# Sums of squares of the second half on the matrix engine, and another order of variances, modulation parts and turns

## What is computed

```python
mod = (silu(c) @ wmod).reshape(2, 6, 1, 1024)          # wmod: 1024 x 6144
sa, ca, ga, sb, cb, gb = (mod[:, i] for i in range(6))  # ga, gb kept away from 0
h = layernorm(x) * (1 + ca) + sa        # mean and variance over the 1024 features
x = x + ga * attn(h)   # per feature: softmax over the 2 batch entries, scores summed over 2048 tokens
h = layernorm(x) * (1 + cb) + sb
x = x + gb * ffn(h)    # silu(h Wgate) * (h Wup), then Wdown; inner width 2752
```

## Time and profile before

| what | us |
|---|---|
| median of 3 runs | 2859.61 |
| lowest and highest run | 2858.69, 2861.7 |
| the profiled execution, its own time | 2868.16 |
| its span, first to last instruction | 2866.0 |
| statistics and modulation, to the start of L1502 | 191.5 |
| PE busy in the span | 2757.2 |
| POOL busy in the span | 157.8 |

### The profile page before, as it was taken

One profiled execution on the slowest core, in us unless ns is written; L12 is line 12 of the kernel. 1 busy time (PEld: TensorE's weight loads), 2 busy tenths in 40 slices (PEclk: granted clock), 3 DMA queues, 4 the chain that ended last, 5 costly groups with the idle time before them and its releaser, 6 DMA issues.

```text
span 2866.0 us, 32548 instructions
## 1 busy us (share of the span) xinstructions
PE 2757.2 (96%) x11784; PEld 2162.9 (75%) x11784; DVE 1547.6 (54%) x2063; ACT 1061.8 (37%) x1622; POOL 157.8 (6%) x206
## 2 busy tenths in 40 slices
PE   8996998989899999999999999999999999999999
PEld 3344877777688887788887788887788888888887
DVE  7787787664445453544453433333546545546444
ACT  4456455544333333333333211111434333333332
POOL 5300010000001101001100000000000000000000
PEclk9997999999999999999999999999999999999999
DMA  8573989888878888978887999999757667667655
GB/s 362 198 299 134 325 297 321 299 282 297 294 276 314 314 283 268 302 279 312 313 285 252 347 348 356 351 352 333 255 211 264 218 220 250 216 224 253 228 208 167
DMA packets 359711, 795.77 MB, mean 278 GB/s; under 512 B 25760, under 2 KB 154016, under 8 KB 350848
## 3 DMA queue, kind: packets, MB, share of 16 engines
q1 hardware_dynamic: 341648, 721.32, 71.8%
q0 software_dynamic: 17088, 59.78, 6.2%
q10 hardware_dynamic: 816, 12.58, 1.0%
HBM read 553.26 MB, written 240.32 MB: 277 GB/s over the span
## 4 chain that ended last, share of the span: by engine, by line
PE 88%; DMA 4%; DVE 3%; issue 2%; ACT 2%; SPq 1%; POOL 1%; DVEq 0%; ACTq 0%; POOLq 0%
PE ps L1547 18%; PE ps L1549 18%; PE ps L1548 18%; PE ps L1609 10%; PE ps L1610 10%; PE ps L1611 10%; PE ps L1426 3%; PE ps L1453 1%; DMA x_raw_P<-xr_dram 1%; DMA whl_dram<-w_lo_P 1%; DMA xbuf<-x 1%; PE ps L1509 0%; PE ps L1502 0%; DMA wm<-wmod 0%; POOL sq_pair L564 0%
## 5 line engine op out<-in xcount | busy, mean ns | idle before, releaser
L1547 PE MATMUL ps<-x_hi_P,w_slot 128*128 128x512 f32 (+1 forms) x1848 | 725.3, 392 | 23.9 <-ACT vv L783 11.8
L1549 PE MATMUL ps<-x_hi_P,w_slot 128*128 128x512 f32 (+1 forms) x1848 | 723.8, 392 | 0.0
L1548 PE MATMUL ps<-x_lo_P,w_slot 128*128 128x512 f32 (+1 forms) x1848 | 723.7, 392 | 0.0
L1609 PE MATMUL ps<-hh,w_hi 128*128 128x512 f32 (+1 forms) x1232 | 481.1, 390 | 3.2 <-DVE w_lo L1322 1.9
L1610 PE MATMUL ps<-hl,w_hi 128*128 128x512 f32 (+1 forms) x1232 | 480.8, 390 | 0.0
L1611 PE MATMUL ps<-hh,w_lo 128*128 128x512 f32 (+1 forms) x1232 | 480.0, 390 | 0.0
L1547 PEld LDWEIGHTS ps<-x_hi_P,w_slot 128*128 128x128 f32 (+1 forms) x1848 | 345.1, 187 | 105.0 <-ACT vv L783 13.0
L1549 PEld LDWEIGHTS ps<-x_hi_P,w_slot 128*128 128x128 f32 (+1 forms) x1848 | 344.8, 187 | 78.4
L1548 PEld LDWEIGHTS ps<-x_lo_P,w_slot 128*128 128x128 f32 (+1 forms) x1848 | 345.3, 187 | 77.6
L1322 DVE TENSOR_TENSOR w_lo<-w_raw,w_hi 128x1408 fp32r<-128x1408 f32 x112 | 181.8, 1624 | 211.8 <-ACT w_hi L850 211.8
L1547 PE MATMUL ps<-x_hi_P,w_hi 128*128 128x512 f32 (+1 forms) x616 | 246.1, 400 | 43.7 <-DVE x_lo_P L1130 10.0
(11 more groups left out here) (179 smaller groups left out, 2598.4 us busy)
## 6 DMA issues: line engine op xcount, KB each, us to landing
w_slot<-whl_dram SPq DMA_DIRECT2D x420, 512.0 KB, 6.0
w_raw<-wds_dram SPq DMA_DIRECT2D x64, 704.0 KB, 4.6
hl_raw<-h_dram SPq DMA_DIRECT2D x56, 768.0 KB, 7.0
h_dram<-hb SPq DMA_DIRECT2D x30, 1280.0 KB, 9.6
whl_dram<-w_hi SPq DMA_DIRECT2D x140, 256.0 KB, 3.4
whl_dram<-w_lo_P SPq DMA_DIRECT2D x140, 256.0 KB, 4.0
w_raw<-wdn SPq DMA_DIRECT2D x48, 704.0 KB, 5.0
hl_raw<-h_dram SPq DMA_DIRECT2D x28, 1024.0 KB, 10.5
```

The source lines that it names most:

```text
L1547: mm(bank, hi[:, w], x_hi[name][:, k, :], start=fresh and k == 0, stop=False, skip_group_check=not fresh)
L1548: mm(bank, hi[:, w], x_lo[name][:, k, :], start=False, stop=False, skip_group_check=not fresh)
L1549: ins = mm(bank, lo[:, w], x_hi[name][:, k, :], start=False, stop=k == KH - 1, skip_group_check=not fresh)
L1609: mm(bank, hi[0:n, w], hh[stage % 2][0:n, j, :], start=fresh and j == 0, stop=False, skip_group_check=not fresh)
```

## The change

In round 1 (`t` = 1) POOL no longer adds pairs of squared tiles. PE sums every squared feature tile itself: 8 matmuls a batch in place of 4, waiting for `sq_ready` and releasing ACT's buffers through `sq_pair_used`. Round 0 stays as it was. PE's list of round 1 is reordered: the variances of batch (0,0) stand right behind the means, and one part lies between each two batches (part 4, then 5, then 6), where before four parts stood ahead of the first batch and two between the second and the third. Behind the last batch come parts 7 to 11. Part 12 alone, in place of parts 12 to 15, stands ahead of the turns of groups 0 and 1.

```diff
@@ gpsimd
                     sum_tiles(1, 0)
                     add_squares(0, 0)
                     sum_tiles(1, 1)
-                else:
-                    add_squares(0, 0)
-                add_squares(0, 1)
-                add_squares(1, 0)
-                add_squares(1, 1)
+                    add_squares(0, 1)
+                    add_squares(1, 0)
+                    add_squares(1, 1)
@@ scalar, square()
-                        act.wait_ge(sq_added, t * (4 * NSQ) + (i * NSQ + j + 1))
+                        if t:
+                            act.wait_ge(sq_pair_used, t * (4 * NSQ) + (i * NSQ + j + 1))
+                        else:
+                            act.wait_ge(sq_added, i * NSQ + j + 1)
@@ tensor, variances()
                     for j in range(NSQ):
-                        pe.wait_ge(sq_added, t * (4 * NSQ) + (i * NSQ + j + 3))
+                        if t:
+                            pe.wait_ge(sq_ready, t * (4 * NSQ) + (i * NSQ + j + 1))
+                            for k in range(SQ_PER):
+                                ins = mm(ps_var[h], ones[:], sq[:, j % 2, k, :], start=j == k == 0, stop=j == NSQ - 1 and k == SQ_PER - 1)
+                            ins.then_inc(sq_pair_used, 1)
+                            continue
+                        pe.wait_ge(sq_added, i * NSQ + j + 3)
                         mm(ps_var[h], ones[:], sq_pair[:, j % 2, :], start=j == 0, stop=j == NSQ - 1).then_inc(sq_pair_used, 1)
@@ tensor, the list of round 1
                     means(1, 1)
-                    parts(0, range(4, GROUP[0]))
-                    parts(1, range(2))
                     variances(0, 0)
+                    parts(0, range(4, 5))
                     variances(0, 1)
-                    parts(1, range(2, 4))
+                    parts(0, range(5, GROUP[0]))
                     variances(1, 0)
+                    parts(1, range(1))
                     variances(1, 1)
-                    parts(1, range(4, GROUP[1]))
+                    parts(1, range(1, GROUP[1]))
 
             pe.wait_ge(eye_loaded, 16)
             pe.wait_ge(centred, 16)
-            parts(2, range(4))
+            parts(2, range(1))
             turn(0, ps_mod[0], ROWS[0] + ROWS[1], 0)
             turn(1, ps_mod[0], ROWS[0] + ROWS[1], ROWS[0])
-            parts(2, range(4, GROUP[2]))
+            parts(2, range(1, GROUP[2]))
             parts(3, range(GROUP[3]))
```

## The result

The changed kernel takes 2869.65 us (median of 8 runs, 2866.5 to 2871.43), the kernel before beside it 2862.18 (8 runs, 2858.69 to 2865.6, the three shown ahead among them): 7.5 us more. The ratio is 1.0022, with a 95% interval of 1.0013 to 1.0030. Slower, by a quarter of a percent: little, but the interval lies clear of 1.

A forecast was written before the change was run, and what follows sets the result against it. The matrix engine's work up to the modulation's end was taken as the bound: 191.0 without stall, plus 6.1 idle and 2.7 lower clock, gives 199.8 against 191.5. That is +8.3 us, 2867.9 from 2859.6; range 2859.0 to 2871.0.

The forecast's parts named there:

- Part 1, the sums: Round 1 sums of squares: four batches take 28.5 us on the matrix engine against 22.3, costing +6.2 us.
- Part 1, VectorE's time: Without GpSimd's additions, five slow VectorE multiplications speed up; the 5.7 us freed are no gain while VectorE is ahead.
- Part 2, the order: Reordered round 1: last batch ends at 129.8 against 134.2, first pair's store issued at 138.8 against 147.01.
- Part 3, the turns: Both turns move from behind part 15 to behind part 12: same 2.4 us of work, nothing saved on the matrix engine.
- The sum without a stall: With no tile late, the modulation ends at 191.0, 0.5 us sooner than before.
- Part 4, the collision: The 4 MB store delays tile 12 to 13.0 us after issue; the matrix engine idles 6.1 us before part 12.
- The reckoning by equal turns: If DMA engines alternate between queues by packet, tile 12 lands at 150.2: stall 3.1 us, +5.3 in all; not adopted.
- The clock: After the idle before part 12 the matrix engine's clock falls to 1.2 GHz, costing 2.7 us as before.
- B: Rival: milder collision, stall of 1 to 3 us or clock not lowered, +2 to +5.5 us; chance 0.17.
- C: Rival: tile 12 lands in time despite the store, nothing idles, clock stays, -0.5 us (2859.1); chance 0.13.
- D: Rival: second tile late or squares can't keep up with the matrix engine, 3 us or more on top; chance 0.07.
- E: Rival: path runs through VectorE, whose chain ends 6 to 8 us sooner; over 6 us faster (2853); chance 0.05.

The follow-up runs named there:

- experiment 1: Kernel before with only the round 1 sums of squares moved to the matrix engine, old order kept: +8.6 us, ratio 1.0028 against the kernel before.
- experiment 9: Changed kernel with the late store, GpSimd still adding round 1 pairs that nobody uses while ScalarE waits for them: +0.3 us, ratio 0.9998 against the kernel before.
- experiment 7: Changed kernel with the turns put back behind part 15: +7.1 us, ratio 1.0024 against the kernel before.
- experiment 6: Changed kernel with the turns ahead of part 12, in the idle gap: +5.7 us, ratio 1.0019 against the kernel before.
- experiment 3: Changed kernel with the first pair's 4 MB store in round 1 issued behind the last modulation tile: -1.6 us, ratio 0.9992 against the kernel before.
- experiment 4: Kernel before with the first pair's 4 MB store in round 1 issued behind the last modulation tile: -4.2 us, ratio 0.9985.
- experiment 8: Changed kernel with one of the store's two chunks (2 MB) issued behind the last tile: +2.4 us, ratio 1.0011 against the kernel before.

## Why the prediction was right

The forecast was 2867.9 against 2859.6, +8.3; measured, +7.5 (2869.65 against 2862.18: with eight runs in place of three the kernel before is itself 2.6 us higher). By the start of the means of `x_f` it is 7.8. The chain of steps held.

- **Part 1, the sums.** Forecast 28.5 us for four batches; they took 7.0 and three times 7.1 on the path (98.10 - 91.14, 129.94 - 122.88), 28.1. That the engine has no idle time to hide them is shown by experiment 1.
- **Part 1, VectorE's time.** Forecast to be worth nothing; experiment 9 shows it, for the kernel with the late store.
- **Part 2, the order.** Last batch at 129.9 (129.8), store at 139.45 (138.8). What the prediction left unsaid is that the order by itself gains 2.9 us of start: it hides GpSimd's first two additions behind a part (2.4 us) and drops the wait of 0.50 ahead of the turns. The change gives the first of these up by its first half.
- **Part 3, the turns.** Worth nothing as the change places them (experiment 7), 2.2 us of start in the gap (experiment 6). The 2.4 us that the prediction calls their work hold the 0.50 of waiting shown in the earlier trace rows; they take 1.9.
- **The sum without a stall.** Forecast 191.0, and 190.51 in experiment 3: the batches took 0.4 less, the turns 0.5 less, the 20 parts 0.5 more than reckoned.
- **Part 4, the collision.** Tile 12 landed 13.0 us after its issue, as taken from tile 16; idle 6.26 (6.1). That close a hit is partly luck: with store and tile placed the same, it took 12.9 in experiment 6 and 14.3 in experiment 7, where the idle of 7.60 lies beyond the upper bound of 6.5. Tile 13 landed at 157.2 (157), without a second stall. The reckoning by equal turns, 150.2, was too early: it landed at 153.5. Experiments 3, 4 and 8 show the store as the cause.
- **The clock.** 5.67 - 3.45 = 2.2 us in place of 2.7: the term that was sized too high, by a fifth. The lowered stretch was shorter after the restart, 153.6 to 158 in place of 161.2 to 166.
- **A slip in the signs to look for.** "L1464 with 16 records only" should be 32: round 0 keeps 16 matmuls, and each is two records. The after trace has 32 there and the 64 of the new line.

The rivals: B's milder stall is what experiment 8 makes, C's schedule is what experiment 3 makes by moving the store away, and ends at 190.51 against the 191.0 of that case; with the store in place it did not come. D and E did not come.

## What to carry to other kernels

Before work is moved to the engine on the critical path, write down that engine's gapless sum: here it rose to within 0.5 us of the old total by the forecast, and within 1.0 as measured (190.51 against 191.47), with every wait removed, so next to nothing could be gained. When a reordering moves a large store, lay its issue beside the issues of the small ring transfers: their distance and the number of steps of slack decide about a stall, whatever the engines' shares say. A bulk store with no early reader belongs where the transfers beside it have slack (here 4 to 9 us on the median for one moved store: 4.2 in the kernel before, 4.6 on top of the order, 9.1 in the changed kernel), and what it meets in the new place has to be looked at too.

## What the hardware showed that I had not expected

- Behind a gap of only 2.29 us the granted clock went from 1.00 to 0.50 (experiment 8), and it went down after the engine had restarted: at work again from 149.37, 1.00 up to 150, 0.52 from there.
- A 1 MB load issued 1.05 us behind the 4 MB store on the other queue waits almost for the whole of it: it lands 14.05 us behind the store's issue, and the store itself 15.8. Each 2 MB of store add about 4.1 us to its landing (4.8, 9.0, 13.0), though the transfers move 328 to 492 GB/s all the while. What in the transfers makes the tile come so late, the runs don't show.
- The same collision is not the same each time: 12.9, 13.0 and 14.3 us in three executions with the store 1.05 us ahead of the tile.
